# A fused attention and mixture-of-experts kernel: expert 0 worked in two entries, the first of them directly behind the attention

## What is computed

```
x = x + tanh(g_xattn) * attention(layernorm(x), ctx, ctx)      # 32 query heads, 8 key heads, d = 32
logits = layernorm(x) @ w_cls.T                                # 64 choices, the first 32 are real experts
topk_idx = top_k(softmax(logits) + bias, 8)
pos = position of a token in its expert's list, in token order  # kept if pos < CAP = 512
y = (silu(x_e @ w_gate) * (x_e @ w_up)) @ w_down               # per expert, 1024 -> 512 -> 1024
x = x + tanh(g_ffn) * (weighted sum of a token's y)
```

## Time and profile before

| | us |
|---|---|
| median of 3 runs | 2343.18 (2337.95 to 2346.47) |
| the profiled execution | 2343.49 |
| its span, first to last instruction | 2341.8 |
| TensorE busy | 2106.2 (90%) |
| VectorE, ScalarE, GpSimd busy | 1436.8, 1218.3, 1050.9 |
| HBM traffic | 176 GB/s over the span |

### The profile page before, as it was taken

One profiled execution on the slowest core, in us unless ns is written; L12 is line 12 of the kernel. 1 busy time (PEld: TensorE's weight loads), 2 busy tenths in 40 slices (PEclk: granted clock), 3 DMA queues, 4 the chain that ended last, 5 costly groups with the idle time before them and its releaser, 6 DMA issues. The chain is left out here.

```text
span 2341.8 us, 47982 instructions
## 1 busy us (share of the span) xinstructions
PE 2106.2 (90%) x14528; PEld 1219.3 (52%) x14529; DVE 1436.8 (61%) x2442; ACT 1218.3 (52%) x1798; POOL 1050.9 (45%) x1228
## 2 busy tenths in 40 slices
PE   5999999999998419899999999999999999999987
PEld 2554544454454214356556664644656676554465
DVE  6788888888886632346446572743564775452474
ACT  3787777776774313235445463633554664353364
POOL 3127888878887560123322441521252534231252
PEclk9999999999999759999999999999999999999999
DMA  5577766676664724567676693955694986765583
GB/s 145 142 175 175 188 165 162 165 194 154 158 151 114 184 70 126 149 160 200 185 188 187 170 259 97 277 178 141 167 251 126 265 233 178 190 177 171 148 213 78
DMA packets 557659, 401.47 MB, mean 171 GB/s; under 512 B 211158, under 2 KB 478550, under 8 KB 557584
## 3 DMA queue, kind: packets, MB, share of 16 engines
q1 hardware_dynamic: 495648, 327.79, 51.2%
q0 software_dynamic: 45184, 72.10, 13.0%
q10 hardware_dynamic: 16752, 0.65, 0.5%
HBM read 310.94 MB, written 101.06 MB: 176 GB/s over the span
## 5 line engine op out<-in xcount | busy, mean ns | idle before, releaser
L1584 PE MATMUL psum<-xgt,wgu 128*128 128x256 f16 (+3 forms) x6144 | 887.0, 302 | 32.4 <-DVE xgt L1335 22.3
L1584 PEld LDWEIGHTS psum<-xgt,wgu 128*128 x6144 | 558.4, 98 | 360.7 <-issue 42.7
L770 POOL TENSOR_TENSOR spare<-spare 128x1 f32<-128x1 f32 x160 | 130.0, 813 | 927.5 <-PE psum L1593 447.3
L1593 PE MATMUL psum<-wdn,apair 128*128 128x512 f16 x1944 | 455.8, 385 | 29.8 <-ACT ys L994 20.0
L1101 DVE TENSOR_REDUCE mx<-psum 128x2 f32<-128x512 f32 x512 | 327.4, 683 | 91.3 <-PE psum L1439 84.4
L1335 DVE COPY xgt<-psum 128x1024 f16<-128x1024 f16 x256 | 167.5, 683 | 269.3 <-PE psum L1569 235.5
L705 POOL DMA_INDIRECT lists<-entry,dest x256 | 281.5, 1100 | 109.9 <-issue 68.5
L1345 DVE SCALAR_TENSOR_TENSOR a<-psum,sg 128x512 f32<-128x512 f32 x128 | 88.3, 690 | 385.8 <-PE psum L1584 371.6
L894 ACT ACTIVATE prob<-psum 128x512 f32<-128x512 f32 x512 | 276.9, 597 | 66.5 <-PE psum L1452 42.8
L1252 DVE SCALAR_TENSOR_TENSOR wgu<-wraw,wgu 128x1024 f16<-128x1024 f32 x256 | 308.6, 1217 | 4.2 <-ACT wgu L911 4.0
L1593 PEld LDWEIGHTS psum<-wdn,apair 128*128 128x128 f16 x1944 | 186.5, 99 | 231.5 <-issue 36.2
(11 more groups left out here) (154 smaller groups left out, 1927.2 us busy)
## 6 DMA issues: line engine op xcount, KB each, us to landing
wraw<-in_L_ffn_w_gate_up_dram SPq DMA_DIRECT2D x256, 512.0 KB
wraw<-in_L_ffn_w_down_dram SPq DMA_DIRECT2D x128, 512.0 KB
x<-in_x_dram SPq DMA_DIRECT2D x16, 1024.0 KB
xr<-in_x_dram SPq DMA_DIRECT2D x16, 1024.0 KB
out_dram<-x SPq DMA_DIRECT2D x16, 1024.0 KB
pairs<-xs SPq DMA_DIRECT2D x16, 1024.0 KB
qs<-qh SPq DMA_DIRECT2D x248, 64.0 KB
qs<-ql SPq DMA_DIRECT2D x128, 64.0 KB
```

The costliest lines, as they stand in the source:

```text
L1584: mm = pe.matmul(ps_gu[:, s, h, 0:nt * P], w[:, a, k, :], xgt[:, c, k, 0:nt * P], start=(k == 0 and (a, c) == (0, 0)), stop=(k == KB - 1 a ...
L1593: mm = pe.matmul(psum[:, Y_BANK[i] + n2, :], apair[:, o, k, c * P:(c + 1) * P], w[:, a, k, :], start=(k == 0 and (a, o) == (0, 0)), stop=( ...
```

## The change

Expert 0 gets two entries, so there are nq = 33 entries instead of 32. Entry 0 holds its tokens of the first cut = 12 batches, entry 1 ("late") those of the last four; both use expert 0's weights, which are loaded twice. The lists get room for one more entry.

- The list of entry 0 is complete when batch 11 is scattered. Its gather stands in step 15, its transposes in slots 3 to 6 of step 15 on TensorE and its copies in the same slots on VectorE.
- The zero fill of `xg` (so far in step 17) stands in step 14 on VectorE.
- The barrier is gone. TensorE goes from the last attention step straight to the products of entry 0; what is left of the router on TensorE (`counts` of batch 14, `logits` of 15, `counts` of 15) stands between the halves of the up products (`up_first`, written out instead of a loop).
- Weight chunks 0 and 1 of entry 0 are loaded at the end of step 15, the other four at the end of step 16. Splits, silu and products with it (`gu_hi`, `gu_lo`, `silu`, `gate_up`, `act_hi`, `act_lo`, `dn_hi`, `dn_lo`) stand written out in the drain steps on ScalarE and VectorE.
- Gather of the late entry: behind `scatter_first`; the other 19 scatters stand behind it, and the gather of expert 1 waits for all of them.

```
+    nq = ne + 1
+    cut = nb - LATE_BATCHES
...
+        def weights_of(e):
+
+            return 0 if is_first(e) else e - 1
...
                 if at_step(b, nb - 1):
                     sp.wait_ge(q_in[1], 192 * nb)
+                    sp.wait_ge(k_in[0], 32 * nb)
                     sp.wait_ge(k_in[1], 32 * nb)
-                    for i in range(4):
+                    for i in range(2):
                         weights(0, i)
                 if at_step(b, nb):
                     sp.wait_ge(t_full, 32 * nb)
-                    for i in range(4, CHUNKS):
+                    for i in range(2, CHUNKS):
                         weights(0, i)
...
                 if is_first(e):
-                    first_wait(sp)
+                    for i in range(CHUNKS):
+                        weights(1, i)
+                    for half_out in lists_out:
+                        sp.wait_ge(half_out, 8 * T2 * TOPK * (nb - 2))
+                    sp.wait_ge(first_out, 2 * 16 * T2)
+                    get_gslots(1, 1)
+                    sp.dma_start(slots[:, 1], lists_v[1]).then_inc(slots_in[1], 16)
+                    for half_out in lists_out:
+                        sp.wait_ge(half_out, 8 * T2 * TOPK * nb)
+                    get_gslots(2, 0)
+                    return
...
+                    if kv == 1 and at_step(b, nb - 1):
+                        gather_first()
+                    elif kv == 1 and on(b, -4) and not early(b):
...
-            gather(0, 0)
+            gather(1, 1)
             scatter(nb - 2, nb % 2, 13, T2 * TOPK)
             scatter(nb - 1, 1 - nb % 2, 0, T2 * TOPK)
             for half_out in lists_out:
                 pool.wait_ge(half_out, 8 * T2 * TOPK * nb)
-            gather(1, 1)
...
+                    if kv == 3 and at_step(b, nb + 1):
+                        gu_hi(0, 2, 0)
+                        gu_hi(0, 2, 1)
+                        silu(0, 0)
+                        gu_hi(0, 3, 0)
+                        act_hi(0, 0)
+                        gu_hi(0, 3, 1)
+                        silu(0, 1)
+                        act_hi(0, 1)
+                        act.wait_ge(x2_ready, nb)
+                        dn_hi(0, 0)
...
+                    if kv == 7 and at_step(b, nb + 1):
+                        gate_up(0, 2)
+                        act_lo(0, 2)
+                        dn_lo(0, 0)
...
+                    if kv == 2 and at_step(b, nb):
+                        gu_lo(0, 0, 0)
+                        gu_lo(0, 0, 1)
                     if kv == 2 and on(b, -1):
                         residual(b - 1, tally)
...
+                    if 3 <= kv < 7 and at_step(b, nb - 1):
+                        take_t(0, 2 * (kv - 3))
+                        take_t(0, 2 * (kv - 3) + 1)
+                    if kv == 7 and at_step(b, nb):
+                        gu_lo(0, 2, 0)
+                        gate_up(0, 0)
+                        gu_lo(0, 2, 1)
+                        act_lo(0, 0)
...
+            def up_first(j, nt):
+
+                pe.wait_ge(gt_free, 2 * nt + FREE)
+                pe.wait_ge(a32_ready, j - 1 + FREE)
+                for h in range(2):
+                    up_half(j, j % 2, wgu[:, j, h].rearrange("p a (k f) -> p a k f", k=KB), nt, h)
+                    if (j, h) == (0, 1):
+                        counts(nb - 2)
+                    if (j, h) == (1, 1):
+                        logits(nb - 1, (0,))
+                    if (j, h) == (2, 0):
+                        logits(nb - 1, (1,))
+                    if (j, h) == (3, 0):
+                        counts(nb - 1)
```

393 lines of the change are left out of this document (214 added, 179 removed).

## The result

| us | before | after |
|---|---|---|
| median of 20 runs on one chip | 2339.57 (2335.81 to 2346.47) | 2345.18 (2337.64 to 2353.09) |
| profiled execution (span) | 2343.49 (2341.8) | 2343.57 (2341.8) |

After against before is 1.0021, with a 95% interval of 1.0011 to 1.0031. The prediction was 2317, 26 us less than before. No such gain came: by the medians the change costs 5.6 us, by the two profiled executions nothing.

A forecast was written before the change was run, and what follows sets the result against it. TensorE was taken to bound it, idle mainly before expert 1's products (957.29). Down products 57.6 us earlier, then an added empty entry of 33.4, put these at 931.1; 2343.49 - 26.2 = 2317.3, predicted 2317, range 2303 to 2339.

The forecast's parts named there:

- The steps up to the first down product: Attention to expert 0's down products: chain through residual, chunk 2 and VectorE's queue, starting them at 861.5 instead of 919.09.
- The attention: Step 15 on TensorE: 64 added transposes lengthen the attention by 3 us, bounds 0 and 7.6.
- rival 2: Step 15: slow transposes go along into the attention, 21.6 us of waiting; gain 4.6, ending at 2339; chance 0.11.
- 2317.3 + 1.4: Silu and exponential table loads on ScalarE: with the skill page's drain, the sum ends 1.4 us later, given as 2318.6.
- To expert 1: First down product through the late entry to expert 1's products: these start at 931.1 instead of 957.29, 26.2 us earlier.
- From the first down product to the next entry's products ... 2 us less: Down products to late entry: before's 38.2 us, 9.77 us issue stall kept, 2 us less for fewer transposes.
- Late products at 897.7, expert 1's at 897.7 + 33.4: Late entry to expert 1 on TensorE: 33.4 us, taken from a one-block, four-block pair at 1698.96 and 1732.34.
- No row excludes that it costs exactly this: Added empty one-block entry: 33.4 us held possible, since TensorE and not the weights sets it there.
- GpSimd's side: Scatters, then expert 1's gather: list and gather at 900.2, landed at 909, TensorE asking at 915.5; in time by 6 us.
- If expert 1's gather lands after TensorE asks for it: Expert 1's opening: one of three signs named as showing the prediction wrong; landing was forecast at 909, asking at 915.5.
- Whatever the change does to that one moment, 957.29, is what it does to the end: Expert 1's products start at 957.29 before; entries then follow with TensorE full, so that shift carries to the end.
- rival 3: Early entry's written-out products on TensorE: code-loading stalls, 9.8 us each; four make it 32 us more, 2349; chance 0.08.

The follow-up runs named there:

- e6: The changed kernel, unchanged, on the third chip beside the kernel before; 2326.38 us, 1.0068 of before.
- e1: The changed kernel without GpSimd's last 19 scatters (batches 14 and 15), on the second chip; 2311.54 us (one run).
- e4: The changed kernel with 128 further wait instructions at the start of TensorE's program (later code 8 KiB further on), second chip; 1.0096 of before.
- e5: The kernel before, unchanged, profiled on the third chip; 2308.65 us (one run).
- e15: The changed kernel with late entry, VectorE order of e9 and four weight chunks issued before the attention's end as in e11, fifth chip; 1.0005 of before.
- e11: e10 with weight chunks 2 and 3 issued with 0 and 1 before the attention's end, fourth chip; 2298.34 us, 0.9840 of before.
- e8: The changed kernel without the late entry and with 128 waits more at the start of TensorE's program, third chip; 2301.70 us, 0.9964 of before.
- e9: The changed kernel with batch 14's list entries ahead of chunk 2's work on VectorE, 16 scatters left instead of 19, fourth chip; 1.0017 of before.
- e10: e8 (no late entry, padding) with the VectorE order of e9, fourth chip; 2303.76 us, 0.9861 of before.
- e12: The kernel before, its 19 last scatters held until TensorE has made all eight transpose groups of expert 0's opening, fourth chip; 2326.80 us, 0.9962 of before.
- e14: The kernel before with its 19 last scatters issued but bounded so nearly every row is skipped, fifth chip; 0.9999 of before.

## Why the prediction was wrong

**The steps up to the first down product were right.** Predicted and measured: residual of batch 15 796.7 and 796.26; first products 797 to 803 and 802.20, behind an "issue" stall of 10.94 us; pairs stored 819.4 and 819.95; round 2 at 831.8 and 833.53, with TensorE waiting 7.45 us; first down product 861.5 and 861.55, released by the down split. The attention cost 2.1 us where I took 3. That one is in part luck: in e6 it cost 5.7, with 6.58 us of standing still ahead of the early entry's first transposes in step 15, for which the sum had no term. The slow hand-over of rival 2 did not show in step 15. (One sum is off by a tenth: 2317.3 + 1.4 is 2318.7.)

**The step that failed is "To expert 1"**, both of its terms.
- *"From the first down product to the next entry's products ... 2 us less"*, 36.2 us: measured 45.4. The 9.77 us stall that I kept was not there, and 17.65 us of waits for VectorE's copies were. These are the slow transposes of the earlier trace rows. I had a rival for them, but looked for them in the attention; they went with the last burst of scatters, which now stood beside the late entry's transposes. Rival 2 gave a gain of 4.6 us at expert 1, and 4.54 were measured: that is a coincidence of numbers, since its stalls were to be in step 15. Without them (e1, e6) this term is 23.8 and 23.9 us, so there it was set 12 us too high. Rows had shown it: the 29.2 us of the earlier trace rows lie over the scatters of the earlier trace rows.
- *"Late products at 897.7, expert 1's at 897.7 + 33.4"*: measured 45.8. The pair in the earlier trace rows has run through both bodies of the loop already. At the first pass through the loop two stalls come with it, 5.46 us ahead of the transposes and 5.48 us at the branch into the four-block body, together 10.9 of the 12.4 too many; in e1, without scatters, they are 6.22 and 7.58. "No row excludes that it costs exactly this" was a poor bound: the earlier trace rows had 9.77 us at the first pass and the earlier trace rows none.

The two terms are 21.6 us short, and 26.2 - 21.6 = 4.6 is within 0.1 of the 4.54 that was measured. For the second term the kind of stall is known, for the first the cause stays open (below).

**GpSimd's side was mis-sized too.** Expert 1's gather was to be issued at 900.2 and there at 909, 6 us before TensorE asks. It was issued at 905.96. On the first chip it was TensorE's own late opening that held it back (the row at 905.22). In e6, where TensorE is in time, TensorE gets the rows at 917.60, after 17.72 us of waiting. The last of the 19 scatters there, and the first piece of the gather:

```profile
897.93 2.61 POOL L723 DMA_INDIRECT lists<-entry,dest  x1 [0.30 <-issue]
...
906.07 1.06 POOL L749 DMA_INDIRECT xg<-pairs,gslots  x1 [0.55 <-issue]
```

Three terms were wrong. From the first to the last start of the 19 scatters it is 28.6 us (869.31 to 897.93) and not 18 x 1.28 = 23.0, since eight of them last 1.3 to 2.9 us, beside VectorE's splits and products. The gather follows the last scatter's start by 8.1 us, not 5.1. And the rows are there 11.5 us after the first gather is issued, not 8.8. "If expert 1's gather lands after TensorE asks for it" was named as what would make the prediction wrong; it should have been a rival with a price.

**"Whatever the change does to that one moment, 957.29, is what it does to the end"** failed by the same size as what was left: 4.86 us more at the last boundary on the first chip. The eleven traces named under e4 show that this goes by the place of the code, which the change moved. Of rival 3 the kind was right and the place wrong: the written-out products ran without stalls behind their first one, and the jumps between entries had them. The page "Runtime: NRT & Kernel Launch" of the Trainium skill (instruction fetch) says just this of taken branches out of the fetched blocks. The rows agree as far as they go. In the changed kernel two instruction packets of about 16 KB each lie between 937 and 945, around the stall ahead of 944.49, and three between 2288 and 2296; the queue's lines for these two stretches:

```profile
q8 instruction: 2, 0.03, 2.9%
...
q8 instruction: 3, 0.05, 2.3%
```

In e4, without the last stall, it is two packets from 2275 to 2290. The view does not say whose packets they are, so that TensorE waited for them is an inference.

**The base was a special case.** I summed against one chip. There before has 29.2 us in expert 0's opening, on the third and fifth chip 10.05 and 9.6, and by its time the second is like them. The change turns that stall into one of 17.65 us elsewhere; where there is none, it has nothing to win at this place and costs 0.7%.

**Where the expected gain went**, in one sentence each. The early start is real: the first down product comes 57.5 us earlier. But expert 1 can't follow it, since the early entry's work on VectorE, the late chunk 2 and the late entry's gather delay the lists: the last scatter is issued at 861.19 in e5 and at 897.93 in e6, 36.7 us later. The empty late entry costs 14 to 20 us of the way from the attention to expert 1 where its transposes do not stall (137.1 in e15 against 123.5 in e11, 153.7 in e6 against 134.0 in e8) and 31.8 where they do (e9 against e10). In each pair the kernel without the entry has the padding too, and the first pair is from two chips, the fifth and the fourth. The last boundary takes 5 us more. The early entry by itself does pay where before has the stalls: e10 and e11, with their other orders and the padding, take 32 and 38 us less than before there, more than the 26 forecast.

**What stays open.** Why TensorE and VectorE stand still beside the scatters on two chips of five, and not on the others. The weights' transfers (C) are not needed for it: the queues are all but idle in the first chip's hole (share 0.03) and in e12's (0.02 and 0.04). Whether the hand-over, the engines' own instruction streams or something else is slow was not tested. The issuing of descriptors and the rows that they write were not told apart, since e14 ran on a chip without the stalls. That chips and not some other condition make the difference is an inference from five sets of runs, one on each chip; within a set the runs of the kernel before agreed within about 0.5%. How the padding moved the first-pass stalls (9.83 us in e4, 5.93 in e8, 5.81 in e15 without it) was not worked out. Neither was the stall ahead of the early entry's transposes in step 15, nor why e10's and e11's down products run at their pace beside the burst.

## What to carry to other kernels

When work is moved ahead of a stage's end, follow not only the work itself but what it is put in front of: here four operations of the early expert stood on VectorE ahead of list entries that did not need them, and a transfer behind a store that it did not need, and together they cost 17 us of the next expert's start (e15 against e6, two chips). Ask of an entry or a loop body that is added where its first pass jumps to; a row from the steady phase does not price it. And when a stall in the profile of before has several releasers and no cause, price the gain both with it and without, and run before on a second chip.

## What the runs showed that was not expected

- Two kinds of chips: medians of 2339.6 and 2336.0 us on two, 2309.3 to 2309.9 on three, for one program. Between a trace of the first and one of the third, 22.2 of 34.9 us are lost between the attention and expert 1, 19.2 of them in one opening beside back-to-back indirect scatters.
- On the one kind other engines can stand still beside such a burst (10.8 us for a hand-over; 7 matmuls in 10 us in e12), though not in e10 and e11; on the other they keep their pace. The scatters themselves do not tell the kinds apart: beside before's transposes they keep their 1.28 us on both (e5), and where VectorE splits weights single ones last longer on both. One lasts 2.90 us beside the down split on the first chip (850.85, the split from 850.62) and 2.90 us on the third (847.53, the split from 847.30).
- Stalls without a releaser stand at many of TensorE's first jumps (10.5 to 12.3 us into the first products behind the attention, 5.5 to 9.8 us ahead of expert 1 in the kernels of this study) and, in the changed kernel, at the last entry, written out behind the loop; 128 waits at the start of the program made that last one (5.40 us) vanish.
